# Constant multiplies ahead of the position counts in the router stage of a convolution and mixture-of-experts kernel

## What is computed

```python
x = x + conv_ref(ln_c(x), gamma1, beta1, w1, gamma2, beta2, w2, pat)
t = to_tokens(x)                       # [64, 256, 64]
flat = ln_t(t)
logits = flat @ router_w.T             # [16384, 8]
probs = softmax(logits)
topk_probs, topk_idx = top_k(probs, 2)
topk_probs = topk_probs / (sum(topk_probs) + 1e-09)
gates = einsum('nk,nke->ne', topk_probs, one_hot(topk_idx, 8))
h = silu(einsum('nc,ehc->neh', flat, w1)) * einsum('nc,ehc->neh', flat, w3)
y = einsum('neh,ech->nec', h, w2)
x = from_tokens(t + einsum('ne,nec->nc', gates, y), x)
```

## Time and profile before

| | us |
|---|---|
| median of 3 runs | 846.76 (845.3 to 847.84) |
| profiled execution | 847.52 |
| its span, first to last instruction | 845.7 |
| TensorE busy | 781.7 (92%) |
| VectorE busy | 564.9 (67%) |
| GpSimd busy | 541.7 (64%) |
| ScalarE busy | 475.4 (56%) |
| granted TensorE clock, mean | 0.926 |

### The profile page before, as it was taken

One profiled execution on the slowest core, in us unless ns is written; L12 is line 12 of the kernel. 1 busy time (PEld: TensorE's weight loads), 2 busy tenths in 40 slices (PEclk: granted clock), 3 DMA queues, 4 the chain that ended last, 5 costly groups with the idle time before them and its releaser, 6 DMA issues.

```text
span 845.7 us, 17377 instructions
## 1 busy us (share of the span) xinstructions
PE 781.7 (92%) x4893; PEld 446.4 (53%) x4893; DVE 564.9 (67%) x1460; ACT 475.4 (56%) x1031; POOL 541.7 (64%) x567
## 2 busy tenths in 40 slices
PE   8999978887699999999999999999999999999833
PEld 6664455555344554545454554545455447777622
DVE  5977576887656666666666666667667666766545
ACT  5516455665156666666666666666666566666400
POOL 3630027777757777777777777777777777777510
PEclk9979977777799999999999999999999999999955
DMA  6460000000144434333333434334343346666278
GB/s 231 82 118 0 1 9 28 28 26 28 36 145 122 131 112 126 116 113 114 112 116 111 122 114 118 116 111 115 111 116 111 114 134 178 193 173 183 66 261 335
DMA packets 62147, 96.76 MB, mean 114 GB/s; under 512 B 13685, under 2 KB 35374, under 8 KB 62096
## 3 DMA queue, kind: packets, MB, share of 16 engines
q1 hardware_dynamic: 41808, 70.48, 28.1%
q0 software_dynamic: 19136, 21.54, 9.1%
q10 hardware_dynamic: 1152, 4.19, 1.2%
HBM read 69.84 MB, written 22.58 MB: 109 GB/s over the span
## 4 chain that ended last, share of the span: by engine, by line
PE 86%; DVE 6%; DMA 2%; issue 2%; SPq 2%; POOL 0%; ACT 0%; DVEq 0%; POOLq 0%
PE bank L1314 40%; PE bank L1329 22%; PE bank L1214 9%; PE bank L1295 3%; PE bank L1239 2%; PE bank L1145 2%; PE bank L1158 2%; PE bank L1287 2%; SPq L429 2%; DMA conv_all<-result_rows 2%; PE bank L1163 2%; PE bank L1174 1%; PE bank L1232 1%; PE bank L1149 1%; PE bank L1252 1%
## 5 line engine op out<-in xcount | busy, mean ns | idle before, releaser
L495 POOL DMA_INDIRECT expert_rows<-y_and_rows,slot_all x256 | 248.9, 972 | 141.1 <-issue 77.2
L1076 DVE TENSOR_TENSOR conv_all<-conv_all,bank 128x512 f32<-128x512 f32 x340 | 233.7, 688 | 151.4 <-ACT conv_all L662 150.4
L1314 PE MATMUL bank<-xT,w 64*128 64x512 f32 (+1 forms) x1608 | 324.6, 534 | 0.0
L662 ACT ACTIVATE conv_all<-bank 128x512 f32<-128x512 f32 x340 | 203.0, 597 | 116.8 <-PE bank L1314 116.6
L1314 PEld LDWEIGHTS bank<-xT,w 64*128 64x128 f32 x1608 | 144.0, 186 | 169.5 <-DVE conv_all L1076 85.7
L505 POOL DMA_INDIRECT result_rows<-conv_all,dest_all x142 | 139.9, 985 | 56.1 <-issue 41.8
L1329 PE MATMUL bank<-conv_all,w 128*64 128x256 f32 x1240 | 161.7, 384 | 1.2 <-DVE tile_map L1045 1.2
L1329 PEld LDWEIGHTS bank<-conv_all,w 128*64 128x64 f32 x1240 | 91.1, 136 | 51.7 <-issue 12.7
L673 ACT ACTIVATE xT<-bank 64x256 f32<-64x256 f32 x272 | 102.8, 378 | 18.7 <-PE bank L1287 16.4
L1214 PE MATMUL bank<-quant_padded,conv_w_blocks 128*128 128x512 bf16 x288 | 78.2, 437 | 0.0
L505 POOL DMA_INDIRECT result_rows<-squares,dest_all x64 | 63.0, 985 | 20.3 <-issue 19.6
(11 more groups left out here) (227 smaller groups left out, 848.1 us busy)
## 6 DMA issues: line engine op xcount, KB each, us to landing
w<-in_w SPq DMA_DIRECT2D x68, 384.0 KB
w<-in_w2t SPq DMA_DIRECT2D x68, 192.0 KB
conv_all<-expert_rows SPq DMA_DIRECT2D x56, 136.0 KB
w_second<-in_w SPq DMA_DIRECT2D x12, 384.0 KB
x_all<-in_x SPq DMA_DIRECT2D x8, 512.0 KB, 4.3
x_all<-y_and_rows POOLq DMA_DIRECT2D x16, 256.0 KB, 3.8
expert_rows<-y_and_rows,slot_all POOLq DMA_INDIRECT x256
y_and_rows<-result_rows SPq DMA_DIRECT2D x8, 512.0 KB, 9.7
```

Source lines behind the costliest of these rows:

```text
L495: nc.gpsimd.indirect_dma_start(xs, bass.IndirectOffsetOnAxis(ap=slot_all[:, s, k * GH + g:k * GH + g + 1], axis=0), rows_all[:, s, g, :], ...
L662: nc.scalar.activation(sbuf[k % 3], h1_ps[k % 3][:], ACT.Silu).then_inc(silu_rdy, 1)
L1076: V.tensor_tensor(hbuf[k], sbuf[k % 3], h3_ps[k % 3][:], ALU.mult).then_inc(mul_rdy, 1)
L1314: ins = mm(ps[k % 3][:, rows_], w[half, cols], xT[u][half, rows_], start=True, stop=True)
```

## The change

In the router stage TensorE calls `keep_busy` ahead of its wait for the one-hot rows of a pair: sixteen multiplies ahead of the first pair's positions, eight ahead of each of the other seven, behind the transposes of the next pair where there are any. They write bank 6, which the stage doesn't use otherwise. Nothing else is changed.

```diff
             def route(p, first=False, last=0):
                 if first:
+                    keep_busy(16, bank[6])
                     positions(p)
                 if last != 1:
                     turn_rows(p + 1)
                 if not first:
+                    keep_busy(8, bank[6])
                     positions(p)
                 if last != 1:
                     logits(p + 1)
```

## The result

The changed kernel takes 838.67 us (median; 837.26 to 840.06) beside 846.63 us for the kernel before in the same comparison: a ratio of 0.9906, with a 95% interval from 0.9879 to 0.9933. The profiled execution after took 839.97 us (span 838.2). One execution of the kernel before, among those beside the last experiments, took 937.43 us at a mean clock of 0.807; it enters no ratio.

What follows compares the result with a forecast made beforehand. The router stage was taken as bound by a VectorE-TensorE ring of 14.0 us a step, slowed by half-clock stretches. From 847.52 us, + 0.3 - 1.2 - 2.0 - 1.2 = - 4.1 gave 843.4 us, range 839.5 to 847.9.

Steps and rivals of the forecast that it cites:

- A new idle stretch of about 2.4 us: Pairs 2 to 5: TensorE's gained time reappears as idle behind the convolution, up to the next transposes, about 2.4 us.
- Half the steps each way: Pairs 2 to 5: half the steps gain the 1.0 us wait, half stay as long: 2.0 us gained in four.
- bad step: Step of pairs 2 to 5 where the clock falls: eights at half, VectorE loses 1.1 us and gains 1.0.
- The first pair's 0.3 us: First pair: the sixteen multiplies end after the one-hot rows, so its positions come late, costing 0.3 us.
- GpSimd's slack: GpSimd's waiting, 6.0 us at the first result scatter and 8.1 near the end, lets some 4 us pass whole.
- Pair 1: Pair 1's waits for squares and convolution: gain between 0 and 5.1 us, taken as 1.2.
- Pairs 2 to 5: Four steps of 14.0 us, 13.0 without the wait: 2.0 us gained, ends 4.1 gained and 4.8 lost.
- Pairs 6 and 7: Pair 6's waits for the convolution give 1.2 us, ends 0 and 2.8; pair 7's eights are hidden, nothing.
- I leave the sum where it is: Whole kernel: sum starts from the profiled 847.52 us, not shifted for the three runs' median, 846.76, 0.8 lower.
- It doesn't do what it says: Rival, router stage: clock still falls in the logits, only the first pair's cost remains, 847.8 us; chance 0.20.
- Slower: Rival, router stage: eights run at half in every step, delaying positions, 1.2 us lost a step, 852.6 us; chance 0.07.
- Full throughout: Rival, router stage: the clock stays full throughout, 11.7 us gained, 835.8 us; chance 0.08.

Runs made afterwards that it cites:

- narrow multiplies: Kernel before plus the same 72 multiplies in the same places, 16 columns each instead of 512: 844.89 us, ratio 0.9979; 40 ahead of the last pair's positions: 844.71 us.

## Why the prediction was right and wrong

**The mechanism was right in the main.** The eights fill the idle ahead of the positions, the waits for the convolution shrink (11.8 to 3.5 us), and with narrow multiplies, which fill nothing, the stage doesn't move at all. "A new idle stretch of about 2.4 us" behind the convolution was measured at 2.4 in pairs 2 and 3 (1.9 to 2.5 in the steps of pairs 2 to 5), and behind it the clock does fall in some steps. Half the steps each way was the count in four of five traces: two short ones and two about as long as before (one and three in the fifth).

**What runs at half in a bad step was wrong.** "Where the clock falls because of it, the eight run at half: they end 1.9 + 3.47 = 5.4 us after the sum" did not happen in any of the five traces. The clock falls one group of multiplies earlier: the sixteen transposes take 3.60 us instead of 2.05 in pair 3, and the eight behind them run mostly at full (1.9 to 2.8 us, nowhere 3.47). That the positions begin 5.2 us after the second sum all the same (155.09 to 160.28) is luck, and with it the price of a bad step came out nearly right: VectorE waits 0.8 to 1.05 us in these steps, where it was to lose 1.1.

**The first pair's 0.3 us** measured 0.13: L944 to L950 took 2.66 us after, and 2.53 before. Pair 7's eights cost nothing that shows: its positions still have 5.73 us of idle ahead of them, against 7.53. GpSimd's slack sufficed: of the 6.0 us at the first result scatter 1.2 were left in the trace of the result and none in the other four, and the 8.1 us near the end sank to 5.0 and 6.4 in the two with the short pair 1, but the tiles followed the earlier stage in all.

**Pair 1 was mis-sized.** "Ends 0 and 5.1; I take 1.2, nearer to the low end by that row of 1.96 us": the row of the later steps was the wrong measure. Where the clock lasts, pair 1 gives 4.7 us, where it doesn't, 0.9, and it lasted in two of five executions of the changed kernel; the mean is 2.4, against the 0.9 taken with the first pair's cost. A term with two outcomes was given one value close to the worse.

**Pairs 2 to 5: the count held, the size of one did not.** A step without its wait was put at 13.0 us, "14.0 - 1.0". It takes 12.7 (12.67 to 12.81). The sums of L888 start 0.80 us apart (141.62 and 142.42), where the late one had started 1.93 behind the first; and from the second sum to the one-hot rows it takes 3.28 us instead of 3.51, because one of the quantiser's operations in between (L852) took 0.42 us there and 0.63 before, in pair 2. The gain is 1.2 to 1.34 us for each short step, not 1.0. A step in which the clock fell takes 13.5 to 14.0, on average 0.2 us less than before, where "stays as long as it is" was expected. Of the 0.7 us beyond the forecast 0.3 come from the short steps, 0.4 from the others.

**Pairs 6 and 7** gave 1.5 us where 1.2 was taken.

**The end was left out.** The sum has no term for it and gives no reason; it is 1.1 to 1.6 us shorter in each of the five traces than in the trace of the kernel before that the table shows, 1.2 in the mean, and also in kernels whose stage didn't change. Why stays open.

**"I leave the sum where it is" took one execution for the kernel.** The prediction saw that falls of the clock elsewhere make the spread, but drew its range from three terms of the stage and started from the profiled 847.52. From the median of the comparison, 846.63, the same range would begin at 838.6 instead of 839.5, just below the measured 838.67. The first one-hot rows come at 111.69 to 114.55 us in different executions of the changed kernel and at 111.87 and 113.73 in those of the kernel before. In the pair of executions compared here that is 2.0 us of the 7.4; over five executions it is 0.8, and nothing says that the change makes it.

Taken together, over five executions: 1.5 us more from pair 1, 0.7 from pairs 2 to 5, 0.3 from pair 6, 1.2 from the end and 0.8 from ahead of the stage, less 0.3 behind the stage and 0.1 in the tiles, make up, to rounding, the 4.2 us between the forecast and the 8.3 us by which the span is shorter.

**The rivals.** "It doesn't do what it says" is refuted by the narrow multiplies' trace beside the change's. "Slower" needed a loss of 1.2 us beyond the gain in every step; the bad steps took no longer than before (13.5 to 14.02 us against 14.01), since the clock rises again by the time of the eights and the convolution behind them runs at full. "Full throughout" is what both stretches filled gave, not the change.

## What to carry to other kernels

Work that fills an engine's idle time must be followed one turn further: the time that it gives back reappears as another idle, and of the fillings tried only that of both kept every step short (833.25 us instead of 838.67). Fill to just below the idle and no further, for filler that outlasts it costs the engine that waits behind it, with the clock full (13.9 us a step instead of 12.7). Look at which engine's slack the gain eats: GpSimd's went from 8.1 us near the end to 1.5. Where a kernel's clock falls differently from run to run, give such a term its two outcomes with their shares, read several executions before one trace is taken as the kernel, and start the sum from the median.

## What the runs showed of the hardware

The clock's falls are not the same in executions of the same program: the kernel before took pair 1 in 22.22 and in 18.58 us, both times behind an idle of 3.79 us, the change in 21.34 and in 17.52, both times behind one of 2.43. And with 72 narrow multiplies, or 40, which left every step of the stage as it was, the end of the kernel was 1.2 and 1.4 us shorter than in the first trace of the kernel before, some 600 us later, in the waits for transfers; no trace here shows why.
